# Time mixing with token shares applied to h, one product each for key, receptance and value, in a three-layer hybrid kernel

## What is computed

```python
# time mixing on h = LayerNorm(LayerNorm(x)), prev = h one token earlier, 0 for the first
k = (h * tmk + prev * (1 - tmk)) @ Wk.T
v = (h * tmv + prev * (1 - tmv)) @ Wv.T
r = (h * tmr + prev * (1 - tmr)) @ Wr.T
x = x + (sigmoid(r) * wkv(decay, first, k, v)) @ Wo.T
```

## Time and profile before

| | us |
|---|---|
| median of 3 runs (lowest, highest) | 508.76 (507.75, 509.42) |
| the profiled execution | 507.94 |
| its span, first to last instruction | 505.6 |
| PE / DVE / ACT / POOL busy in the span | 470.4 / 391.0 / 360.3 / 360.6 |
| start of slot 0 (the first product of its `logits`) | 138.8 |

### The profile page before, as it was taken

One profiled execution on the slowest core, in us unless ns is written; L12 is line 12 of the kernel. 1 busy time (PEld: TensorE's weight loads), 2 busy tenths in 40 slices (PEclk: granted clock), 3 DMA queues, 4 the chain that ended last, 5 costly groups with the idle time before them and its releaser, 6 DMA issues.

```text
span 505.6 us, 10587 instructions
## 1 busy us (share of the span) xinstructions
PE 470.4 (93%) x3662; PEld 322.8 (64%) x3662; DVE 391.0 (77%) x1051; ACT 360.3 (71%) x711; POOL 360.6 (71%) x445
## 2 busy tenths in 40 slices
PE   3787999998599999999999999999999989999994
PEld 2555788997256666665565765666566756666663
DVE  5897999777376687889888898888887868477664
ACT  1789999874375867976696958694886566868552
POOL 4564676788276658789879879888889586466652
PEclk9999899999599999999999999999999999999999
DMA  8102011000010000000000000000000000000000
GB/s 275 38 3 87 8 32 33 1 2 3 6 63 0 2 1 2 2 2 1 1 2 1 1 1 1 1 2 3 0 1 22 2 1 23 0 2 1 22 1 21
DMA packets 7012, 8.49 MB, mean 17 GB/s; under 512 B 560, under 2 KB 5168, under 8 KB 6960
## 3 DMA queue, kind: packets, MB, share of 16 engines
q1 hardware_dynamic: 6960, 7.83, 4.8%
HBM read 6.78 MB, written 1.05 MB: 15 GB/s over the span
## 4 chain that ended last, share of the span: by engine, by line
PE 55%; DVE 8%; POOL 5%; ACT 3%; issue 2%; DVEq 0%; POOLq 0%; ACTq 0%
PE bank L1544 9%; PE bank L1548 9%; PE bank L1545 9%; PE bank L1563 5%; PE bank L1565 5%; PE bank L1564 5%; PE bank L1680 3%; PE bank L1663 2%; PE bank L1606 2%; DVE x L1914 2%; PE bank L1607 2%; POOL b_hc L2195 1%; PE bank L1591 1%; PE bank L1570 1%; DVE b_hid L1898 1%
## 5 line engine op out<-in xcount | busy, mean ns | idle before, releaser
L2133 POOL TENSOR_TENSOR b_hid_lo<-b_hid,b_hid_hi 128x512 f16<-128x512 f32 x144 | 167.8, 1177 | 56.7 <-ACT b_hid_hi L1740 54.5
L1898 DVE SCALAR_TENSOR_TENSOR b_hid<-bank,b_silu 128x512 f32<-128x512 f32 x144 | 97.8, 688 | 62.0 <-ACT b_silu L1733 36.7
L1733 ACT ACTIVATE b_silu<-bank 128x512 f32<-128x512 f32 x144 | 85.9, 597 | 58.9 <-PE bank L1548 58.5
L1544 PE MATMUL bank<-x_hi,wsplit 128*128 128x512 f16 x288 | 110.2, 382 | 5.5 <-PEq L130 4.8
L1545 PE MATMUL bank<-x_hi,wsplit 128*128 128x512 f16 x288 | 110.2, 382 | 0.0
L1548 PE MATMUL bank<-x_lo,wsplit 128*128 128x512 f16 x288 | 110.2, 382 | 0.0
L1563 PE MATMUL bank<-wsplit,b_hid_hi 128*128 128x128 f16 x576 | 100.2, 219 | 4.3 <-DVE x L1914 2.6
L1740 ACT CAST b_hid_hi<-b_hid 128x512 f16<-128x512 f32 x144 | 88.2, 612 | 21.9 <-DVE b_hid L1898 21.7
L1565 PE MATMUL bank<-wsplit,b_hid_lo 128*128 128x128 f16 x576 | 100.2, 219 | 0.0
L1564 PE MATMUL bank<-wsplit,b_hid_hi 128*128 128x128 f16 x576 | 100.2, 219 | 0.0
L1914 DVE SCALAR_TENSOR_TENSOR x<-bank,b_w_branch,x 128x128 f32<-128x128 f32 x256 | 71.5, 342 | 16.1 <-PE bank L1565 16.0
(11 more groups left out here) (237 smaller groups left out, 932.6 us busy)
## 6 DMA issues: line engine op xcount, KB each, us to landing
moe_raw<-in_moe SPq DMA_DIRECT2D x9, 384.0 KB, 4.6
x<-in_x SPq DMA_DIRECT2D x4, 256.0 KB, 3.9
out<-x SPq DMA_DIRECT2D x4, 256.0 KB, 2.3
rope<-in_rope SPq DMA_DIRECT2D x1, 512.0 KB, 6.0
wzx<-in_wzx SPq DMA_DIRECT2D x1, 386.0 KB, 6.4
b_w_rkvo<-in_w_rkvo SPq DMA_DIRECT2D x1, 256.0 KB, 2.6
b_w_fk<-in_w_fk SPq DMA_DIRECT2D x1, 256.0 KB, 2.8
b_w_fv<-in_w_fv SPq DMA_DIRECT2D x1, 256.0 KB, 3.6
```

The source lines that it names most:

```text
L1544: nc.tensor.matmul(dst, hi, x_hi[:, q % 2, :], start=True, stop=False)
L1733: nc.scalar.activation(silu[:, 2 * (u % 2) + blk, :], gate_ps[blk][:, :], ACT.Silu, scale=GU_UNSCALE).then_inc(silu_ready, 1)
L1898: nc.vector.scalar_tensor_tensor(hid[:, 2 * (u % 2) + blk, :], up_ps[blk][:, :], GU_UNSCALE * H_SCALE, silu[:, 2 * (u % 2) + blk, :], ALU. ...
L2133: nc.gpsimd.tensor_tensor(hid_lo[:, slot, :], hid[:, 2 * (u % 2) + blk, :], hid_hi[:, slot, :], ALU.subtract).then_inc(lo_ready, 1)
```

## The change

`w_now`, `w_prev` and `mixes` go (six small POOL instructions). For each sequence POOL makes `step_h` = h minus prev (`step`), DVE makes `shared_h[:, j]` = `step_h` times share plus prev, three instructions (`share`), and `project` is one product with the plain weight. Two of the shares stand behind `scan_max` on DVE, the first a unit earlier. ACT's `copy_h` waits until DVE has made all three shares of the sequence before.

```diff
 def project(j, bank, made):
-    nc.tensor.matmul(bank[:, :], w_now[:, j, :], hT[:, 1:SEQ + 1], start=True, stop=False)
-    nc.tensor.matmul(bank[:, :], w_prev[:, j, :], hT[:, 0:SEQ], start=False, stop=True).then_inc(made, 1)
+    nc.tensor.matmul(bank[:, :], w_rkvo[:, j, :], shared_h[:, j, :], start=True, stop=True).then_inc(made, 1)
...
 def copy_h(s):
     act.wait_ge(h_turned, s + 1)
+    if s:
+        act.wait_ge(shared_ready, 3 * s)
...
+def share(s, j):
+    made, which = ((k_made, 0), (r_made, 2), (v_made, 1))[j]
+    dve.wait_ge(step_ready, s + 1)
+    if s:
+        dve.wait_ge(made, s)
+    nc.vector.scalar_tensor_tensor(shared_h[:, which, :], step_h[:], col(core, ("tmk", "tmv", "tmr")[which]),
+                                   hT[:, 0:SEQ], ALU.mult, ALU.add).then_inc(shared_ready, 1)
...
+def step(s):
+    if s == 0:
+        pool.wait_ge(zeroed, 1)
+    else:
+        pool.wait_ge(shared_ready, 3 * s)
+    pool.wait_ge(hT_ready, s + 1)
+    nc.gpsimd.tensor_tensor(step_h[:], hT[:, 1:SEQ + 1], hT[:, 0:SEQ], ALU.subtract).then_inc(step_ready, 1)
```

The tables of `beside` change on all four engines, some 45 entries by one place up to four units. Two lines of PE's and two of DVE's:

```diff
-                    if at == (16, 1):
+                    if at == (15, 1):
                         turn_h(s)
...
-                    if at == (26, 0):
+                    if at == (26, 1):
                         turn_c(s)
...
+                    if at == (16, 1):
+                        share(s, 0)
                     if at == (17, 0):
                         scan_max(s)
-                    if at == (17, 1):
+                        share(s, 1)
+                        share(s, 2)
                         carry(s)
                         difference(s)
```

More of the change, by code:

```diff
@@ L1460, in phase_body @@
         hT = sb("hT", [P, SEQ + 1])
+        step_h = sb("step_h", [P, SEQ])
+        shared_h = sb("shared_h", [P, 3, SEQ])
         pp = sb("pp", [P, SEQ + 1])
@@ L1623, in receptance @@
             def receptance(s):
+                pe.wait_ge(shared_ready, 3 * s + 2)
                 pe.wait_ge(normT_ready, s + 2)
@@ L1687, in beside @@
                 q, e = divmod(u, BRANCHES)
-                if (e, place) == (0, 1) and q < SLOTS:
+                if (e, place) == (0, 0) and q < SLOTS:
                     logits(q)
@@ L1825, in beside @@
                 if q + 1 < SEQS:
+                    if (e, place) == (4, 2):
+                        apply_x(q + 1, (0, 1))
                     if (e, place) == (7, 2):
-                        apply_x(q + 1, (0, 1))
-                    if (e, place) == (7, 3):
                         apply_x(q + 1, (2, 3))
                 elif q + 1 < SLOTS:
-                    if (e, place) == (7, 2):
+                    if (e, place) == (8, 0):
                         apply_x(q + 1, (2, 3))
@@ L2053, in beside @@
                 q, e = divmod(u, BRANCHES)
-                if (e, place) == (0, 2):
+                if (e, place) == (0, 0):
                     route_shift(q)
-                if (e, place) == (0, 2):
+                if (e, place) == (0, 0):
                     route_first(q)
@@ L2059, in beside @@
                     route_second(q)
-                if (e, place) == (1, 2):
+                if (e, place) == (2, 0):
                     route_weigh(q)
-                if (e, place) == (7, 0) and SEQS <= q + 1 < SLOTS:
+                if (e, place) == (7, 2) and SEQS <= q + 1 < SLOTS:
                     apply_x(q + 1, (0, 1))
-                if (q, e, place) == (1, 6, 1):
+                if (q, e, place) == (0, 2, 0):
                     stats(ln_m1, x, SEQS - 1)
-                if (q, e, place) == (1, 6, 2):
+                if (q, e, place) == (1, 0, 1):
                     aggregate(ln_m1, SEQS - 1, veps_in)
@@ L2211, in beside @@
                 q, e = divmod(u, BRANCHES)
-                if (u, place) == (3, 0):
-                    mixes()
-                if (e, place) == (8, 0) and q + 1 < SLOTS:
+                if (e, place) == (7, 1) and q + 1 < SLOTS:
                     low_x(q + 1)
-                if (q, e, place) == (1, 8, 0):
+                if (q, e, place) == (1, 2, 2):
                     pool.wait_ge(veps_in, 1)
```

112 lines of the change are left out of this document (52 added, 60 removed).

## The result

The kernel became slower. Four runs each, taken side by side: 508.25 us before (506.19 to 509.42), 514.68 us after (513.9 to 518.54), ratio 1.0137 with a 95% interval of 1.0104 to 1.0171. Forecast were 498.1 us and a range of 493 to 504. The profiled execution of after took 513.92 us, 6.0 more than that of before.

A forecast was written before the change was run, and what follows sets the result against it. The prediction took PE's work as the bound, with 9.0 us of waits in slots 2 to 5. Twelve products removed gave 10.3 us, waits falling to 8.6 us gave 0.4: 508.76 - 10.7 = 498.1 us, range 493.0 to 504.0.

The forecast's parts named there:

- The waits for `b_hc`: PE's transposes waiting for this buffer: they go once turn_c moves one place later, 2.3 us over four sequences.
- The table loads: On ACT in slot 1: two more loads of 1.28 us for the decay's exponential, within idle time, counted 0.
- POOL's waits ahead of `low_x`: low_x, a unit earlier, can wait for x_hi up to a unit: covered, 0; without cover 1.2 us a slot.
- A stall of 0.5 us: At k = 17 PE's up waits for the first b_hid, behind two shares, carry and difference; 2.0 us for four sequences.
- The room of 3.25 us: At k = 17 before the change: time from the end of the first b_hid to PE's next up half.
- PE's next two units hold `hidden`, `gate_c` and all of `values`: Behind POOL's packed denominator and numerator (k = 20 and 21): PE work of 6.5 and 9.5 us, so no low part late.
- the stall at k = 19 and 20: PE's up waits for ACT and DVE, 0.7 to 1.6 us, taken as 1.1 three times and 0.3 once; together 3.6.
- The 2.4 us for `b_hn` and for the first share at `key`: Stalls kept after turn_h, apply_h and copy_h move a unit forward: 0.3 us each, four times each.
- the 8.6 forecast: PE's waits in slots 2 to 5 after the change, 8.6 us instead of 9.0: 2.0 + 3.6 + 2.4 + 0.6.
- A: Rival: DVE becomes the bound, all shares taking 1.70 us beside busy POOL, slots 2 to 4 longer; 512.3 us, chance 0.07.
- B: Rival: part of the gain; stalls of 1.5 us at k = 17 and 1.6 at k = 19; 503.6 us, chance 0.20.
- D: Rival: at the projections the second product was free, PE would have waited for DVE anyway; 508.8 us, chance 0.05.

The follow-up runs named there:

- e4: The changed kernel's order with the old arithmetic: two products for each projection, no step and no share; 508.46 us, ratio to before 0.998 to 1.002.
- e12: The changed kernel's order with a share for key alone; receptance and value keep two products each; 508.30 us, ratio to before 0.9984 to 1.0019.
- e2: The changed kernel with the second and third step of POOL's denominator moved one and two places later; 519.30 us.
- e11: The changed kernel with two of POOL's denominator steps computed for one column only; 514.79 us.
- e8: The changed kernel with the shares of receptance and value computed for one column only in sequences 1 to 3; 511.84 us.
- e13: The changed kernel's order with shares for key and receptance (the latter at (17, 2)), two products for value; 508.97 us.

## Why the prediction was wrong

**What held.** PE is the bound in most units and its products cost what the rows said: 0.86 us each (the one at 264.70 in after is followed by the next product at 265.56), twelve gone. Shares cost DVE 14.2 us in sum, 1.2 each, from 0.75 to 1.73; forecast were 14.4, from 0.74 to 1.75:

```profile
L2000 DVE SCALAR_TENSOR_TENSOR b_shared_h<-b_step_h,cols,b_hT 128x512 f32<-128x512 f32 x12 | 14.2, 1206 | 0.3
```

The waits for `b_hc` went. Units 27 to 35 take 49.6 us. The table loads cost nothing that shows. POOL's waits ahead of `low_x` grew from 5.9 to 14.9 us; no wait of PE's is put down to them.

**"A stall of 0.5 us" at k = 17: the term that failed most.** It was 3.72 us in unit 36. The room of 3.25 us was right for before. Against the forecast's 3.7 us on DVE, three things went wrong. The pair cost 3.2 us from start to start, not 2.45: I let one share run undisturbed in a gap of POOL, and POOL filled the gap (in sequence 1 it did not, and there the pair takes 1.41 us). `carry` behind it took 1.56 and not the 0.66 of the earlier trace rows; I had taken its old duration as its own property, and it was short only because POOL paused (e4, e12). And DVE came to the scan 1.4 us later than before (2.06 us behind unit 35's start, before 0.69), because `step` and key's share delay POOL's `ln_moe_rstd`, on which `apply_x` waits (e12 against e4), and the new order has put `apply_x` just ahead of the scan; I had costed these two where they stand and not for what queues behind them. 0.75 + 0.9 + 1.4 is 3.0 of the 3.2 us between 0.5 and 3.7. In sequences 0 and 1 units 18 and 27 show no such wait; there the units ahead hold less mixing, and the shares of the pair and `carry` take 0.75 us each. So 2 x 3.7 us of waiting and not 4 x 0.5.

**The clock: not in the sum at all.** 3.0 us in unit 36, nearly as much as the wait itself, 1.7 in unit 45 and 1.2 in unit 22: 5.9 us. The earlier trace rows show 1.00 in each slot, where the longest wait of PE was 1.3 us (`b_hc`), and I took the clock as given.

**"PE's next two units hold `hidden`, `gate_c` and all of `values`".** That was the cover for POOL's packed `denominator` and `numerator`, and it is true from slot 3 on. In slot 2 no sequence is in channel mixing yet: that of sequence 0 starts at k = 29, in slot 3. There the cover is missing: 6.3 us in unit 22, of the 8.1 lost in slot 2. I walked slot 3 and charged slot 2 with slot 3's answer. With the order alone 4.7 of the 6.3 are there already (e4: 9.59 against 4.9), the rest comes with the shares. Why the shares lengthen it is not split further, and spreading `denominator` (e2) and shortening it (e11) did not free the unit.

**Too high: the stall at k = 19 and 20.** Forecast were 3.6 us. Against their own work units 19, 20, 28, 29, 37, 38, 46 and 47 lose 1.4 us together, 0.7 of them in unit 38. The 2.4 us for `b_hn` and for the first share at `key` came out right: 2.6 in the eight units of k = 15 and 16.

**Small ones.** Unit 13 takes 1.1 us more: `ln_moe`'s root on POOL has moved from unit 17 to unit 11 and stands, for 1.5 us, between two low parts for which PE's `down` waits. Slot 0 takes 1.1 us more, at a low clock in either kernel. Both were taken as 0. And one reading of the earlier trace rows was off: PE is busy for 96% of slot 2 (44.46 of 46.17 us), not for 97 or more.

The balance: 16.2 us more lost than the 8.6 forecast, and 514.68 - 498.1 = 16.6. The waits at k = 17 make 5.4 of it (7.4 for 2.0), the clock behind them 4.7, unit 22 with its clock 6.3; all the rest took 6.4 us where 6.6 were forecast.

**The rivals.** A gave 512.3, the nearest of all, and had the mechanism, DVE's instructions waiting for POOL's beside them; e8 shows it directly. That the time came near is in part luck, since neither the clock nor unit 22 is in its sum. It was wrong in form: no slot is bound by DVE's sum (50.3 of 57.4 us in slot 4), three single waits do it. Its point of decision, that more than 3.8 us of DVE's idle time stay, was met (53.53 - 48.97 = 4.6 us in slot 3). What spoke against it in the text, "a longer DVE queue fills by itself" the idle pieces, is what failed. My reading of it, not shown by a run of its own: DVE's late `b_hid` stops PE, PE's stop brings the next input late, and so the idle time is kept. B priced the pair at 3.5 us, near to the 3.2 measured, and was too cheap all the same, since it left `carry` and the late start out. D came out closer than I gave it: with two thirds (e13) or one third (e12) of the shares taking out the second product leaves the median where it was.

**What is open.** Whether some order of these steps turns part of the 10.3 us into time. Sixteen kernels did not: none is faster than before by more than its interval. e13's profiled execution took 506.3 us, but its median is 508.97 (506.06 to 510.03). A search over many orders wasn't made.
